# Leaving out the 45 dummy products per image on TensorE in an attention-and-FFT image block

## The chip, the cores and the metric

The kernel runs on one core of a Trainium2 chip. TensorE multiplies, VectorE (DVE), ScalarE (ACT) and GpSimd (POOL) work element by element, SyncE (SP) issues the transfers. The metric is the device time of one execution in microseconds: the median of the runs shown. [...]

## The reference

The input is eight images of 384 channels and 64 x 64 pixels. Two layers follow each other, each with a group norm before it and a residual after it:

```
x = x + linear_attention(group_norm(x))      # layer 0
x = x + fft_conv_gate(group_norm(x))         # layer 1

# layer 0, per image; q and k get rotary factors, 6 heads of 64
q = elu(rope(Wq x + bq) / 8) + 1 ;  k = elu(rope(Wk x + bk)) + 1 ;  v = Wv x + bv
kv = k^T v (per head) ; ksum = sum of k over pixels
out = Wfc (q kv / (q ksum + 1e-6)) + bfc

# layer 1, per image
t = W_in x ; t = irfft2(rfft2(t in 8x8 patches) * filter) ; t = depthwise 3x3(t)
out = W_out (gelu(t[:192]) * t[192:])

# group norm: 32 groups of 12 channels, mean and variance over channels and pixels
```

## The kernel before, in words

The images run one after the other in an unrolled program, and each is cut into 8 chunks of 512 pixels. An image has three parts.

Part A (`part_a`) takes each chunk in four tiles of 128 pixels. `project` multiplies the normalised image, split into a high and a low half (x_hi, x_lo), with the query, key and value weights (lines L1136, L1137, L1141). DVE turns (`rope`), ACT takes exponentials, POOL adds, DVE finishes the key tile (`elu`, L853), and `add_kv` (L1164) adds the product of keys and values, with the key sums in one column more, into one PSUM bank over the whole image.

Then comes the *key-value seam*. DVE copies the key sums (`ksum`, L883), makes diagonal matrices of them (`kdiag`, L887), and fixes the key-value matrix up (`kvfix`, L891, L895). TensorE spreads the key sums over all partitions with a product of ones (L1198); ACT copies that out as `kbc` (L607). TensorE transposes the fixed matrix (L1202), ACT copies it (L609), TensorE multiplies it by Wfc (L1207), and ACT and DVE split that into `mout_hi` and `mout_lo`. Beside it, POOL and DVE multiply the first chunk's queries by `kbc` (L474, L944), DVE sums them per head and takes reciprocals (L906 to L910), DVE and POOL divide (L917, L481), and TensorE transposes the divided queries (L1217).

Part B (`part_b`), the output stage, multiplies the transposed queries by `mout` for each chunk (L1238, L1246). DVE adds bias and residual and takes the statistics of the sum (L936, L968). POOL's divisions L481 come once per chunk.

Then comes the *statistics seam*, `group_norm` on DVE and `group_avg` on TensorE. Per channel means and variances are averaged over the channels of a group by two small products of two columns each (L1124): the first on the means (`mv`), read back in L794, the second on variance plus squared deviation (`dev`), read back in L799. DVE and ACT make the scale and the shift (L801 to L806), DVE normalises the first chunk for layer 1 (L823), ACT rounds it to x_hi (L567), DVE takes x_lo (L1027).

Part C (`part_c`) is layer 1: the projection (again L1136, L1137, L1141), the transform to the patch basis (L1283), the filter on DVE (L987), the way back (L1290), the taps of the depthwise convolution on ACT, POOL, DVE and TensorE (L1007, L1317), gates, and the output product (L1302 to L1306). Part A of the next image begins at its end.

Every engine takes its instructions in the written order and waits on semaphores, so a product that waits holds up all that are written behind it. `keep_warm` (L1113) writes products whose result nobody reads, of 128 rows by 512 columns, into a bank that is free at that time. They wait for nothing themselves. In each image 6 stand ahead of the last `add_kv`, 4 ahead of L1198, 2 ahead of L1202, 10 ahead of the first transposes of part B, 14 ahead of the first small product of `group_avg`, 2 ahead of its second, and 7 ahead of the first product of part C.

Of the kernel before, what the change touches and what calls it, by code (L numbers as in the profile page):

```python
# [10 lines left out]
P = 128  # L11
KB = C // P
CHUNK = 512
NCH = NTOK // CHUNK
# [98 lines left out]
def build_program(nc, x, wqkv_t, bqk, bv, wfc_t, bfc, filt, w_in_t, w_dw, w_out_t,  # L113
# [11 lines left out]
    with ctx:  # L125
        def sb(name, shape, dt=fp32):
            return ctx.enter_context(nc.sbuf_tensor(name, shape, dt))
# [12 lines left out]
        w_hi = sb("w_hi", [P, KB, 3 * C], fp32r)  # L140
# [5 lines left out]
        win_hi = sb("win_hi", [P, KB, C], fp32r)  # L146
# [64 lines left out]
        bank = [ctx.enter_context(nc.psum_tensor(f"bank{j}", [P, 512], fp32)) for j in range(8)]  # L211
# [75 lines left out]
        def steps(total, body):  # L287

            for c in range(total):
                body(c, c // 2, c, c % 2)  # L290

        def within(edge, a, b, off=0):

            return edge is None or a <= edge + off < b
# [810 lines left out]
        def _(pe):  # L1105
# [1 line left out]
            pe.wait_ge(s_cst, NCST * 16)  # L1107
            nc.tensor.matmul(bank[6][:, 0:C], sel, fsel[:, :], start=True, stop=True).then_inc(s_filter, 1)

            def keep_warm(n, free):  # L1110

                for _ in range(n):
                    nc.tensor.matmul(bank[free][:, :], win_hi[:, 0, 0:P], w_hi[:, 0, 0:CHUNK], start=True, stop=True)  # L1113

            def group_avg(f, n_warm=0, free=0):

                for step, (wait, src) in enumerate(((1, lambda k: mv[:, :, k, 0]), (4, lambda k: dev[:, :, k]))):
                    if step == 1:
                        keep_warm(n_warm, free)
                    pe.wait_ge(s_gs, f * 11 + wait)  # L1120
                    for m in range(KB):
                        ks = [k for k, mm in GBLOCKS if mm == m]
                        for k in ks:
                            ins = nc.tensor.matmul(bank[7][:, 2 * m:2 * m + 2], t_gavg[:, GBLOCKS.index((k, m)), :], src(k),  # L1124
                                                   start=(k == ks[0]), stop=(k == ks[-1]))
                    ins.then_inc(s_gp, 1)

            group_avg(0)
            pe.wait_ge(s_split, 2)

# [13 lines left out]
            def project(T, m, par, j, blocks=range(3)):  # L1144

                p2 = j % 2
                pe.wait_ge(s_rope, T + 1)
                pe.wait_ge(s_v, T + 1)
                tok = slice(j * P, (j + 1) * P)
                for b in blocks:  # L1150
                    dst = bank[ABANK[p2][b]][:, 0:C]
                    cols = slice(b * C, (b + 1) * C)
                    ins = split_product(dst, lambda k: x_hi[:, par, k, tok], lambda k: x_lo[:, par, k, tok],
                                        lambda k: w_hi[:, k, cols], lambda k: w_lo[:, k, cols],
                                        m if j == 0 and b == 0 else None)
                    ins.then_inc(s_qkv, 1)

            def add_kv(T, j, first=False, last=False, frees=False):

                pe.wait_ge(s_elu, T + 3)  # L1160
                pe.wait_ge(s_v, T + 3)
                p2 = j % 2
                for k in range(KB):
                    ins = nc.tensor.matmul(bank[KVB][:, k * (P + 1):(k + 1) * (P + 1)], kt[:, p2, k * P:(k + 1) * P],  # L1164
                                           vt[:, p2, k, :], start=(first and k == 0), stop=last, skip_group_check=True)
                    if frees and k == 0:
                        ins.then_inc(s_xfree, 1)
                ins.then_inc(s_kv, 1)
# [3 lines left out]
            for i in range(images):  # L1172

                def part_a(c, h, edge, par):
                    T = (i * 8 + c) * 4
                    first = edge == 0
                    m = i * 16 + c
                    project(T + 2, m, par, 2)
                    if first:
                        pe.wait_ge(s_res, i * 48 + 6)  # L1180
                    add_kv(T, 0, first=first)
                    project(T + 3, m, par, 3)
                    add_kv(T + 1, 1, frees=True)
                    if within(edge, 0, NCH, 1):
                        project(T + 4, m + 1, 1 - par, 0)
                    add_kv(T + 2, 2)
                    if within(edge, 0, NCH, 1):
                        project(T + 5, m + 1, 1 - par, 1)
                    if edge == NCH - 1:
                        keep_warm(6, 0)  # L1190
                    add_kv(T + 3, 3, last=(edge == NCH - 1))

                steps(NCH, part_a)


                keep_warm(4, 5)
                pe.wait_ge(s_kd, i * 5 + 2)
                nc.tensor.matmul(bank[0][:, 0:C], ones_r[:, :].bitcast(fp32), kdiag[:, :, :], start=True, stop=True).then_inc(s_kp, 1)  # L1198
                keep_warm(2, 5)
                pe.wait_ge(s_kd, i * 5 + 4)  # L1200
                for j in range(KB):
                    ins = nc.tensor.transpose(bank[1][:, j * P:(j + 1) * P], kvfix[:, j], ident)  # L1202
# [7 lines left out]
                def transpose_q(c, par, blocks=range(KB)):  # L1210
                    n = i * 8 + c
                    pe.wait_ge(s_qn, n + 2)
                    pe.wait_ge(s_qnp, n + 2)
                    for j in blocks:
                        pe.wait_ge(s_ql, n * 3 + (j + 1))
                        for u in range(TPC):
                            ins = nc.tensor.transpose(bank[(par + j) % 2][:, u * P:(u + 1) * P],  # L1217
                                                      qn[:, par, u, j * P:(j + 1) * P], ident)
                        ins.then_inc(s_tp, 1)

                keep_warm(10, 5)
                transpose_q(0, 0)
                pe.wait_ge(s_ka, i * 5 + 5)
                pe.wait_ge(s_mlo, i * 3 + 3)
# [35 lines left out]
                    if more:  # L1260
                        transpose_q(c + 1, 1 - par, (2,))
                steps(NCH, part_b)
                keep_warm(14, 0)
                group_avg(i + 1, 2, 0)
                keep_warm(7, 0)


                pe.wait_ge(s_split, 3)
# [139 lines left out]
```

## Time and profile before

| | us |
|---|---|
| median of 3 runs | 3549.17 |
| lowest, highest | 3548.68, 3550.89 |
| the profiled execution | 3545.66 |
| span of its trace | 3543.9 |

The profiled execution is one more run, 3.5 us below the median of the others. The span runs from its first to its last instruction. Of the span TensorE is busy 94%, DVE 84%, POOL 58%, ACT 49%. An image takes about 434 us. In this text image 0 is the first, and image 1 has its key-value seam near 668 us and its statistics seam near 750 us of the span.

In the trace's rows a time is microseconds from the span's start. Matmuls are pipelined, and each is shown with its own latency, so that two neighbours overlap; a product of fp32 operands has two records. Idle time before an instruction stands in brackets, with what ended it.

### The profile page before, as it was taken

What the parts mean: (1) busy time and instruction counts of PE and PEld (TensorE: products, weight loads), DVE (VectorE), ACT (ScalarE), POOL (GpSimd) and SP (SyncE); (2) the same over time, 40 slices, a digit from 0 to 9 for tenths busy, and PEclk for the clock granted to TensorE, in tenths of its full rate; (3) what the DMA queues carried; (4) which work ended last, traced back from release to release, by engine and by line L of the source; (5) the groups of instructions that cost most, each with busy time, mean ns of one, the idle gap of its engine ahead of it and who ended that gap; (6) DMA issues with size and microseconds to landing.
All of it is one profiled execution on the core that took longest, in us unless ns stands there. A gap on an engine that the chain in (4) does not pass through costs nothing. (4 is left out here: it accounts for less than half of the span.)

```text
span 3543.9 us, 50201 instructions
## 1 busy us (share of the span) xinstructions
PE 3318.6 (94%) x17374; PEld 2872.3 (81%) x17374; DVE 2981.3 (84%) x5231; ACT 1723.4 (49%) x3159; POOL 2042.9 (58%) x1343
## 2 busy tenths in 40 slices
PE   5999999999999999999999999998999999999998
PEld 4987779877797778977789777896779967799775
DVE  7877989779898798887989879888798887888887
ACT  2433854338443474435744257442664426644275
POOL 2555755547556475564755647456565565655665
PEclk9999999999999999999999999999999999999999
DMA  6215332143321432123332233213332133331422
GB/s 224 72 36 178 106 109 72 54 161 107 122 67 63 143 132 100 63 85 125 130 101 70 90 133 124 100 54 111 113 125 99 54 131 113 113 101 52 143 99 98
DMA packets 185341, 369.89 MB, mean 104 GB/s; under 512 B 7771, under 2 KB 8835, under 8 KB 184835
## 3 DMA queue, kind: packets, MB, share of 16 engines
q1 hardware_dynamic: 185090, 366.68, 30.3%
q8 instruction: 142, 2.33, 0.3%
q14 instruction: 109, 0.88, 0.1%
HBM read 265.99 MB, written 100.66 MB: 103 GB/s over the span
## 5 line engine op out<-in xcount | busy, mean ns | idle before, releaser
L1136 PE MATMUL bank<-w_hi,x_hi 128*128 128x384 f32 x2304 | 803.5, 349 | 17.9 <-ACT vt L578 10.7
L444 POOL TENSOR_TENSOR t<-t 128x768 f32<-128x768 f32 x256 | 535.3, 2091 | 466.4 <-DVE t L841 462.4
L1137 PE MATMUL bank<-w_lo,x_hi 128*128 128x384 f32 x2304 | 781.7, 339 | 0.0
L1007 DVE SCALAR_TENSOR_TENSOR bank<-big,wdw,bank 128x512 f32<-128x512 f32 x1072 | 749.1, 746 | 20.4 <-PE bank L1317 17.3
L437 POOL TENSOR_TENSOR x_lo<-xa,x_hi 128x512 fp32r<-128x512 f32 x360 | 459.4, 1292 | 478.4 <-ACT x_hi L567 478.4
L509 POOL TENSOR_TENSOR prod<-prod 128x512 f32<-128x512 f32 x320 | 410.5, 1283 | 244.5 <-ACT prod L670 224.9
L1141 PE MATMUL bank<-w_hi,x_lo 128*128 128x384 f32 x2304 | 533.1, 339 | 0.5 <-POOL x_lo L437 0.5
L572 ACT ACTIVATE t<-t 128x384 f32<-128x384 f32 x256 | 134.7, 526 | 759.5 <-POOL t L444 747.8
L1136 PEld LDWEIGHTS bank<-w_hi,x_hi 128*128 128x128 f32 x2304 | 436.8, 190 | 23.9 <-issue 22.7
L1137 PEld LDWEIGHTS bank<-w_lo,x_hi 128*128 128x128 f32 x2304 | 437.3, 190 | 1.1
L1141 PEld LDWEIGHTS bank<-w_hi,x_lo 128*128 128x128 f32 x2304 | 415.0, 189 | 1.4 <-POOL x_lo L437 1.4
L836 DVE TENSOR_TENSOR bank<-bank,qkbias 128x384 f32<-128x384 f32 x512 | 279.6, 559 | 137.9 <-PE bank L1141 137.6
L1136 PE MATMUL bank<-win_hi,x_hi 128*128 128x384 f32 x768 | 305.4, 398 | 0.9 <-ACT x_hi L567 0.4
L670 ACT ACTIVATE prod<-big,wdw 128x512 f32<-128x512 f32 x384 | 261.5, 715 | 71.5 <-DVE bank L1007 71.2
L1290 PEld LDWEIGHTS bank<-t_mats,gb 128*128 128x128 f32 x1536 | 205.4, 191 | 89.9 <-issue 35.5
L626 ACT ACTIVATE qt_hi<-bank 128x512 fp32r<-128x512 f32 x192 | 107.4, 594 | 314.8 <-PE bank L1217 314.8
L1137 PE MATMUL bank<-win_lo,x_hi 128*128 128x384 f32 x768 | 259.9, 338 | 0.0
L841 DVE TENSOR_TENSOR t<-bank,t_csw 128x384 f32<-128x384 f32 x512 | 258.4, 545 | 0.0
L1238 PE MATMUL bank<-qt_hi,mout_hi 128*128 128x512 f32 x576 | 247.7, 430 | 0.0
L1164 PE MATMUL bank<-vt,kt 128*128 128x129 f32 x1536 | 214.8, 275 | 25.6 <-DVE kt L853 25.6
L1290 PE MATMUL bank<-t_mats,gb 128*128 128x128 f32 x1536 | 217.1, 277 | 17.8 <-ACT big L640 9.4
L1164 PEld LDWEIGHTS bank<-vt,kt 128*128 128x128 f32 x1536 | 206.9, 190 | 30.6 <-DVE kt L853 30.6
(132 smaller groups left out, 6966.8 us busy)
## 6 DMA issues: line engine op xcount, KB each, us to landing
xr<-x SPq DMA_DIRECT2D x128, 768.0 KB, 4.7
xa<-x SPq DMA_DIRECT2D x64, 768.0 KB, 6.3
x_scratch<-xr SPq DMA_DIRECT2D x64, 768.0 KB, 3.3
xa<-x_scratch SPq DMA_DIRECT2D x64, 768.0 KB, 6.0
xr<-x_scratch SPq DMA_DIRECT2D x64, 768.0 KB, 4.8
out<-xr SPq DMA_DIRECT2D x64, 768.0 KB, 3.3
big<-x SPq DMA_DIRECT2D x8, 768.0 KB, 10.2
w_raw<-wqkv_t SPq DMA_DIRECT2D x1, 1728.0 KB, 6.8
```

The costliest lines, as they stand in the source:

```text
L437: nc.gpsimd.tensor_tensor(dst, src, hi, ALU.subtract).then_inc(s_lo, 1)
L444: nc.gpsimd.tensor_tensor(a, a, b[:, :, ::-1, :], ALU.add).then_inc(s_add, 1)
L509: nc.gpsimd.tensor_tensor(prod[:, 0], prod[:, 0], prod[:, slot_of(q)], ALU.add).then_inc(s_padd, 1)
L670: nc.scalar.activation(prod[:, slot_of(q)].rearrange("p (r s) -> p r s", s=W), filt_img[:, 2, ds(c * ROWS + q // 3, ROWS), q % 3:q % 3 + W ...
L836: nc.vector.tensor_tensor(qk, qk, qkbias[:, b * C:(b + 1) * C], ALU.add).then_inc(s_bias, 1)
L841: ins = nc.vector.tensor_tensor(dst[:, p2, b].rearrange("p s (f r) -> p s f r", r=2), src, tab.unsqueeze(1).unsqueeze(3).to_broadcast(wide ...
L1007: nc.vector.scalar_tensor_tensor(dst, src, wdw[:, k, q:q + 1], so_far, ALU.mult, ALU.add)\
L1136: nc.tensor.matmul(dst, hi(k), whi(k), start=(k == 0), stop=False)
L1137: nc.tensor.matmul(dst, hi(k), wlo(k), start=False, stop=False)
L1141: ins = nc.tensor.matmul(dst, lo(k), whi(k), start=False, stop=(k == KB - 1))
L1164: ins = nc.tensor.matmul(bank[KVB][:, k * (P + 1):(k + 1) * (P + 1)], kt[:, p2, k * P:(k + 1) * P], vt[:, p2, k, :], start=(first and k == ...
L1290: ins = nc.tensor.matmul(bank[INVB][:, k * P:(k + 1) * P], gb[:, p2, k * P:(k + 1) * P], phi_t, start=True, stop=True)
```

## The change

The function `keep_warm` and its seven calls go. `group_avg` loses the two arguments that only fed it. No other instruction is added, taken away or put elsewhere. The lines after it move up by 7 to 14 in the new file.

```diff
-            def keep_warm(n, free):
-
-                for _ in range(n):
-                    nc.tensor.matmul(bank[free][:, :], win_hi[:, 0, 0:P], w_hi[:, 0, 0:CHUNK], start=True, stop=True)
-
-            def group_avg(f, n_warm=0, free=0):
+            def group_avg(f):
 
                 for step, (wait, src) in enumerate(((1, lambda k: mv[:, :, k, 0]), (4, lambda k: dev[:, :, k]))):
-                    if step == 1:
-                        keep_warm(n_warm, free)
                     pe.wait_ge(s_gs, f * 11 + wait)
...
-                    if edge == NCH - 1:
-                        keep_warm(6, 0)
                     add_kv(T + 3, 3, last=(edge == NCH - 1))
 
                 steps(NCH, part_a)
 
 
-                keep_warm(4, 5)
                 pe.wait_ge(s_kd, i * 5 + 2)
                 nc.tensor.matmul(bank[0][:, 0:C], ones_r[:, :].bitcast(fp32), kdiag[:, :, :], start=True, stop=True).then_inc(s_kp, 1)
-                keep_warm(2, 5)
                 pe.wait_ge(s_kd, i * 5 + 4)
...
-                keep_warm(10, 5)
                 transpose_q(0, 0)
...
                 steps(NCH, part_b)
-                keep_warm(14, 0)
-                group_avg(i + 1, 2, 0)
-                keep_warm(7, 0)
+                group_avg(i + 1)
```

TensorE's written order at the key-value seam of the first image, before:

```order
L1164 MATMUL bank<-vt,kt 128x129 x6
L1113 MATMUL bank<-w_hi,win_hi 128x512 x6
L1164 MATMUL bank<-vt,kt 128x129 x3
L1113 MATMUL bank<-w_hi,win_hi 128x512 x4
L1198 MATMUL bank<-kdiag,ones_r 128x384
L1113 MATMUL bank<-w_hi,win_hi 128x512 x2
L1202 MATMUL bank<-t_mats,kvfix 128x128 x3
L1207 MATMUL bank<-wfc,kv_t 128x384 x3
L1113 MATMUL bank<-w_hi,win_hi 128x512 x10
L1217 MATMUL bank<-t_mats,qn 128x128 x12
```

And the same place now, with the new file's line numbers (L1157 is the old L1164, L1188 the old L1198, L1206 the old L1217):

```order
L1157 MATMUL bank<-vt,kt 128x129 x9
L1188 MATMUL bank<-kdiag,ones_r 128x384
L1191 MATMUL bank<-t_mats,kvfix 128x128 x3
L1196 MATMUL bank<-wfc,kv_t 128x384 x3
L1206 MATMUL bank<-t_mats,qn 128x128 x12
```

The four L1113 rows are gone, and the real products follow each other in the same order. At the statistics seam, before:

```order
L1246 MATMUL bank<-qt_lo,mout_hi 128x512 x3
L1113 MATMUL bank<-w_hi,win_hi 128x512 x14
L1124 MATMUL bank<-mv,t_gavg 128x2 x7
L1113 MATMUL bank<-w_hi,win_hi 128x512 x2
L1124 MATMUL bank<-dev,t_gavg 128x2 x7
L1113 MATMUL bank<-w_hi,win_hi 128x512 x7
L1136 MATMUL bank<-win_hi,x_hi 128x384
```

And now (L1234, L1117 and L1129 are the old L1246, L1124 and L1136):

```order
L1234 MATMUL bank<-qt_lo,mout_hi 128x512 x3
L1117 MATMUL bank<-mv,t_gavg 128x2 x7
L1117 MATMUL bank<-dev,t_gavg 128x2 x7
L1129 MATMUL bank<-win_hi,x_hi 128x384
```

Here three L1113 rows are gone, and between the last output product and the first product of layer 1 only the small products of two columns are left.

## Rows read from the trace of the kernel before

**Rows 1.** The page, part 1: busy us (share of the span) xinstructions.

```profile
PE 3318.6 (94%) x17374; PEld 2872.3 (81%) x17374; DVE 2981.3 (84%) x5231; ACT 1723.4 (49%) x3159; POOL 2042.9 (58%) x1343
```

**Rows 2.** The core's span and its mean granted TensorE clock.

```profile
core 0: 3543.9 us, clock 0.981
```

**Rows 3.** Stretches: length, busy us (instructions) per engine, granted clock, DMA share, GB/s.

```profile
668.30:671.70 3.40, 3.40 (x10) 2.41 (x10) 2.17 (x8) 0.00 (x0) 0.00 (x0) 0.50 0.00 1
682.00:685.30 3.30, 3.30 (x10) 2.75 (x11) 2.52 (x4) 0.60 (x1) 1.10 (x1) 0.50 0.02 5
747.00:753.60 6.60, 6.18 (x34) 4.88 (x33) 4.47 (x11) 0.00 (x0) 0.00 (x0) 1.00 0.52 179
753.60:760.50 6.90, 6.71 (x23) 5.16 (x22) 2.97 (x14) 0.97 (x3) 0.00 (x0) 0.51 0.57 204
487.40:490.80 3.40, 3.40 (x13) 3.40 (x12) 3.24 (x7) 1.89 (x3) 1.97 (x2) 0.50 0.48 186
700.00:740.00 40.00, 38.31 (x187) 29.35 (x187) 39.48 (x59) 10.91 (x20) 31.04 (x14) 1.00 0.55 185
1982.40:1989.20 6.80, 6.03 (x17) 4.87 (x17) 5.08 (x7) 1.07 (x2) 4.28 (x3) 0.50 0.00 0
```

The engines stand in the order PE, PEld (TensorE's weight loads), DVE, ACT, POOL.

**Rows 4.** TensorE in order of time, end of image 0: start, length, line, [idle before].

```profile
486.06 0.47 PE L1302 MATMUL bank<-g_hi,wout_hi 128*128 128x512 f32 x1 [3.55 <-DVE xr L939]
```

**Rows 5.** All engines in order of time, key-value seam of image 1.

```profile
668.45 2.06 PE L1113 MATMUL bank<-w_hi,win_hi 128*128 128x512 f32 x4
...
669.10 0.68 DVE L887 TENSOR_SCALAR kdiag<-t_mats,ksum 128x128 f32<-128x128 f32 x3
...
670.30 1.48 PE L1198 MATMUL bank<-kdiag,ones_r 128*128 128x384 f32 x2
...
671.82 0.49 ACT L607 ACTIVATE kbc<-bank 128x384 f32<-128x384 f32 x1 [5.25 <-PE bank L1198]
...
677.55 2.14 POOL L481 TENSOR_TENSOR qn<-big,nrm 128x768 f32<-128x768 f32 x1 [2.57 <-DVE nrm L910]
...
685.62 2.15 POOL L481 TENSOR_TENSOR qn<-big,nrm 128x768 f32<-128x768 f32 x1 [2.52 <-DVE nrm L910]
...
693.93 2.15 POOL L481 TENSOR_TENSOR qn<-big,nrm 128x768 f32<-128x768 f32 x1 [0.55 <-DVE nrm L910]
```

**Rows 6.** The same in image 4.

```profile
1973.10 0.49 ACT L607 ACTIVATE kbc<-bank 128x384 f32<-128x384 f32 x1 [4.04 <-PE bank L1198]
...
1978.82 2.15 POOL L481 TENSOR_TENSOR qn<-big,nrm 128x768 f32<-128x768 f32 x1 [2.57 <-DVE nrm L910]
...
1986.89 2.15 POOL L481 TENSOR_TENSOR qn<-big,nrm 128x768 f32<-128x768 f32 x1 [2.52 <-DVE nrm L910]
...
1996.42 2.15 POOL L481 TENSOR_TENSOR qn<-big,nrm 128x768 f32<-128x768 f32 x1 [0.55 <-DVE nrm L910]
```

**Rows 7.** Statistics seam of image 1, in order of time.

```profile
751.58 1.72 PE L1124 MATMUL bank<-mv,t_gavg 128*128 128x2 f32 x14 [0.42 <-DVE mv L790]
...
754.10 3.15 PE L1124 MATMUL bank<-dev,t_gavg 128*128 128x2 f32 x14
...
757.36 0.17 DVE L799 TENSOR_SCALAR gvar<-bank 128x6 f32<-128x6 f32 x1 [3.31 <-PE bank L1124]
...
760.51 0.41 PE L1136 MATMUL bank<-win_hi,x_hi 128*128 128x384 f32 x1
...
765.01 0.91 PE L1283 MATMUL bank<-tb,t_mats 128*128 128x384 f32 x2 [0.59 <-ACT tb L634]
```

**Rows 8.** The second small product's reader at the statistics seam of image 2.

```profile
1190.37 0.17 DVE L799 TENSOR_SCALAR gvar<-bank 128x6 f32<-128x6 f32 x1 [1.89 <-PE bank L1124]
```

**Rows 9.** Who waited for whom: us in total, times, longest us.

```profile
ACT kbc L607 <- PE bank L1198: 37.4, 8, 5.3
DVE gvar L799 <- PE bank L1124: 27.1, 9, 3.3
DVE gmean L794 <- PE bank L1124: 18.5, 9, 3.3
```

## The prediction

> **What bounds the kernel now.** I read the page's busy shares first. TensorE is busy 94% of the span [rows 1], but that counts pipelined products and the dummies too. So I asked for busy times by stretch. In the middle of the output stage VectorE is busy 39.48 of 40 us, TensorE 38.31 [rows 3]: VectorE sets the pace there, and little on TensorE's side is worth anything. The change touches only the two seams of an image, where this does not hold: the key-value seam, between the last projection and the first output product, and the statistics seam, between the last output product and the first product of the second layer. There one engine works at a time, and small products stand in the chain.
>
> Next, TensorE's granted clock. [...] Even with the dummies it falls at the seams: in image 1 from 668.3 to 671.7 and again from 682.0 to 685.3 as the output stage starts, and at the statistics seam from 753.6 to 760.5 [rows 3]. The mean over the span is 0.981 [rows 2], so low time is about 2 x 0.019 x 3544 = 135 us. A fall also comes with no dummy near: TensorE idles 3.55 us before L1302 at 486.06 [rows 4], and from 487.4 to 490.8 the clock is 0.50 [rows 3]. So idleness brings it down, and the dense work that follows brings it back 3 to 5 us after it begins (682.0 to 685.3, and 486.1 to 490.8). The fall at 487.4 came 4.9 us after that idle stretch began. I reckon with falls 2 to 6 us after dense work ends, an estimate around this one and the others at the seams.
>
> **The change part by part.** Removed are 6 + 4 + 2 + 10 dummies at the key-value seam and 14 + 2 + 7 at the statistics seam, in each of eight images. Nothing is added, and the order of everything else stays. The direct saving is small, since the dummies fill waits. Only where the clock is low do they hold something up: in image 1 the four at 668.45 run low, and L1198 starts at 670.30, though its diagonal was ready at 669.10 + 0.68 = 669.78 [rows 5]. That 0.5 us is in term 1. The others end before what they stand ahead of is ready; L1136 at 760.51 [rows 7] waits for its x_hi anyway. What the change costs is the clock, in five terms.
>
> 1. *The way to the key row, kbc.* The chain is: last key tile, product into the key-value bank, sums, diagonal, L1198, ScalarE's copy L607. From there to the first division on POOL (L481) the way is fixed: 677.55 - 671.82 = 5.73 us in image 1, 1978.82 - 1973.10 = 5.72 in image 4 [rows 5, 6]. ScalarE idles before L607 5.25 us in image 1, where the clock is low, and 4.04 in image 4, where it is not [rows 5, 6]; 37.4 over eight, 4.68 on average [rows 9]. Without dummies only two short products into the bank stand between the projections and L1198, so I expect a low clock in all eight. Of image 1's 5.25, 0.5 goes with the dummies; its low set in at 668.3 only, with the product into the bank partly done (a dummy behind it starts at 668.45), and a wholly low one adds, I estimate, up to 0.6. That makes 5.4. Cost 0.75 x 8 = 6 us. Ends: 0 and 1.1 each, 9.
>
> 2. *Start of the output stage.* TensorE now comes to it low in every image. Image 1 was low for 3.3 us there, and its divisions on POOL follow each other after 8.07 and 8.31 us. Image 4 was low for 6.8 us (1982.4 to 1989.2), and they follow after 8.07 and 9.53 [rows 3, 5, 6]. So a short low is free and a long one costs 1.2; the first kind is the commoner at the seams before. After, between both: 0.5 each, 4 us, less the 1.2 paid already: 2.8. Ends: -1.2 and 8 x 1.2 - 1.2 = 8.4.
> [...]
>
> 3. *First statistics step.* Fourteen records of two columns each take 1.72 us at full clock (751.58) and 3.15 low (754.10) [rows 7]; VectorE waits for them in L794. Over nine such waits it idles 18.5 us [rows 9], 2.06 each, near the 1.89 of a step at full clock (L799 in image 2 [rows 8]): with 14 dummies ahead this step is mostly at full clock. Four dummies take 2.06 us at the low level [rows 5], so about 0.22 each at full clock; 14 of them and the 0.42 idle behind them are some 3.5 us, in which TensorE now does nothing. With falls 2 to 6 us after dense work, about half the images take the step wholly low and most others partly: 1.0 of the 1.43 each, 8.0 us. Ends 0 and 11.4.
>
> 4. *Second statistics step.* VectorE waits 3.31 us before L799 in image 1 (low), 1.89 in image 2 (full), 27.1 over nine [rows 7 to 9]. One of the nine lies ahead of the images and is as long as the longest, 3.3, so eight make 23.8. All low: 26.5. Cost 2.7, nearly fixed.
>
> 5. *Start of the second layer.* The 7 dummies bring the clock back at 760.5, just when the first product comes [rows 3, 7]. Without them real products must do it, in 3 to 6 us. The first 2 us are hidden, since the products wait for x_hi and x_lo. Up to 4 us at half speed then lose up to 2, and TensorE's idle 0.59 before L1283 takes part of it [rows 7]: 0 to 1.5 each. As in term 2 a short low is free and a long one dear; I take 0.7, 5.6 us. Ends 0 and 12. It is kept afterwards, because VectorE only waits here and is the bound later.
>
> Sum: 6 + 2.8 + 8 + 2.7 + 5.6 = 25 us. The profiled execution took 3545.66 us, so 3571 in its terms. The median of the runs stands 3.5 us above it: 3549.2 + 25 = 3574.
>
> **Rivals.** I call a difference real over 0.2%, 7 us: about what a measurement of this kernel can tell from none.
>
> *A. The lows fall where nothing waits.* Image 1's second low was free. Then only term 4 and part of term 1 are left, 3 to 6 us: 3552 to 3555. Against it: at both statistics steps VectorE waits for TensorE with nothing else to do, in every image.
>
> *B. The clock falls from load, and the dummies bring it down.* The lows at 668.3 and 753.6 do set in among dummies [rows 3, 5]. Without them both seams would run at full clock: L607 waits 4.04 instead of 4.68 (-5.1 us), L799 1.89 instead of 2.98 (-8.7), the output stage's 1.2 goes: -15, so 3534, faster. It decides if the seams show 1.00. Against it: rows 4, a fall after plain idleness, and 40 us of dense products at 1.00 in rows 3.
>
> *C. Every low microsecond costs half of one.* By rows 3 the lows at image 1's seams sum to 3.4 + 3.3 + 6.9 = 13.6 us. They would grow to about 27: from the last key tile to some 4 us into the output stage with a recovery between, and from 4 us after its end to 4 us into the next layer. 13 x 8 / 2 = 52 us, 3601. Against it: image 1's low at the output stage cost nothing, and TensorE mostly waits while it is low.
> [...]
>
> **How the numbers follow.** Forecast 0.78, A 0.10, B 0.04, C and all above 3591 0.08. Slower by over 0.2%: 0.86; within: 0.10; faster: 0.04. The range: with terms 1 and 3 at half, 2 and 5 near nothing and 4 whole, 3 + 4 + 2.7 = 10, I go a little below that, to 3556, to take in part of A; with 2, 3 and 5 near their upper ends (5, 3 and 6 more, and 3 for term 1), 3574 + 17 = 3591. So 3556 to 3591.
>
> **What would show it.** Mean clock 0.961 to 0.970, low time some 100 us more than 135. L607's idle about 5.4 us in every image, none near 4.0, 43 over eight. L794's wait for the statistics product grows from 18.5 to about 26, L799's from 27.1 to about 29.8. The second layer's first L1283 comes up to 1.5 us later after L1136. The output stage goes on at 8.3 us a chunk. I am wrong if the statistics steps show full clock, if the added waits are there but the stages behind them shorten by as much, or if the second layer absorbs term 5.

## The result, and the profile after

| | before | changed |
|---|---|---|
| median, us | 3550.03 (4 runs, 3548.68 to 3552.57) | 3578.66 (4 runs, 3577.01 to 3584.52) |
| ratio, 95% interval | | 1.0083 [1.0065, 1.0100] |
| span of the profiled execution | 3543.9 | 3582.7 |
| mean granted clock of TensorE | 0.981 | 0.956 |

The change costs 28.6 us, 0.8%. The profiled execution of the changed kernel was the slowest of its four runs, and that of before stood below its median, so the two traces differ by 38.8 us, ten more than the medians. Up to seven of those ten can be put down to longer waits for loads, shown below.

The page's first lines, to be held against [rows 1]:

```profile
span 3582.7 us, 49481 instructions
PE 3278.2 (91%) x17014; PEld 2850.6 (80%) x17014; DVE 2985.9 (83%) x5231; ACT 1724.6 (48%) x3159; POOL 2042.3 (57%) x1343
```

TensorE lost 360 products and 40 us of busy time, and the other engines have the same number of instructions as before. Stretches of image 1 (its seams now stand 6 and 7 us later), columns as in [rows 3]:

```profile
661.00:673.00 12.00, 7.81 (x50) 7.42 (x48) 8.34 (x18) 4.59 (x9) 4.15 (x2) 1.00 0.19 51
673.00:683.30 10.30, 8.15 (x17) 4.24 (x17) 5.69 (x13) 2.06 (x5) 2.48 (x1) 0.50 0.05 19
683.30:686.70 3.40, 0.96 (x8) 0.86 (x8) 2.37 (x5) 0.63 (x2) 3.20 (x2) 1.00 0.00 0
686.70:693.50 6.80, 5.76 (x18) 4.59 (x17) 5.09 (x7) 1.45 (x3) 4.28 (x2) 0.50 0.00 0
758.40:775.50 17.10, 12.48 (x47) 12.34 (x48) 6.90 (x23) 3.98 (x9) 3.07 (x3) 0.50 0.55 186
```

The lows of 3.4, 3.3 and 6.9 us have become 10.3, 6.8 and 17.1. In this trace the granted clock reads 1.00 or 0.50 in every half microsecond from 662 to 702 us but the four in which it changes (0.56, 0.70, 0.72 and 0.96); 0.50 is what is called low here. The key-value seam is at the low level from the last key tile to the end of the Wfc products, comes back for 3.4 us, in which TensorE is nearly idle, and falls again among the transposes: eight of the twelve begin at 685.74, the last four at 687.85. All engines there, in order of time, against [rows 5]:

```profile
673.40 1.66 PE L1157 MATMUL bank<-vt,kt 128*128 128x129 f32 x6 [3.40 <-DVE kt L853]
...
676.09 1.65 PE L1188 MATMUL bank<-kdiag,ones_r 128*128 128x384 f32 x2 [1.04 <-DVE kdiag L887]
...
677.78 0.49 ACT L607 ACTIVATE kbc<-bank 128x384 f32<-128x384 f32 x1 [5.49 <-PE bank L1188]
...
678.96 4.21 PE L1196 MATMUL bank<-wfc,kv_t 128*128 128x384 f32 x6 [0.58 <-ACT kv_t L609]
...
683.50 2.15 POOL L481 TENSOR_TENSOR qn<-big,nrm 128x768 f32<-128x768 f32 x1 [2.57 <-DVE nrm L910]
...
691.57 2.15 POOL L481 TENSOR_TENSOR qn<-big,nrm 128x768 f32<-128x768 f32 x1 [2.52 <-DVE nrm L910]
...
700.93 2.15 POOL L481 TENSOR_TENSOR qn<-big,nrm 128x768 f32<-128x768 f32 x1 [0.55 <-DVE nrm L910]
```

ScalarE waits 5.49 us for the key row, and the way from there to the first division is 5.72 as before. The Wfc products take 4.21 us instead of 2.20, and that costs nothing: what reads them is due later. POOL's second division follows the first after 8.07 us, and the third the second after 9.36. At the statistics seam of the same image, against [rows 7]:

```profile
758.96 3.15 PE L1117 MATMUL bank<-mv,t_gavg 128*128 128x2 f32 x14 [4.00 <-DVE mv L790]
...
762.22 0.16 DVE L794 COPY gmean<-bank 128x6 f32<-128x6 f32 x1 [3.31 <-PE bank L1117]
...
762.90 3.15 PE L1117 MATMUL bank<-dev,t_gavg 128*128 128x2 f32 x14 [0.79 <-DVE dev L797]
...
766.16 0.17 DVE L799 TENSOR_SCALAR gvar<-bank 128x6 f32<-128x6 f32 x1 [3.31 <-PE bank L1117]
...
769.32 0.66 PE L1129 MATMUL bank<-win_hi,x_hi 128*128 128x384 f32 x1 [3.27 <-ACT x_hi L567]
...
775.22 0.93 PE L1269 MATMUL bank<-tb,t_mats 128*128 128x384 f32 x2
...
776.24 0.56 DVE L987 TENSOR_TENSOR gb<-bank,fsel 128x384 f32<-128x384 f32 x1 [3.71 <-issue]
```

Both small products now take the low 3.15 us. From the first product of layer 1 to L1269 (the old L1283) it is 5.90 us instead of 4.50, and TensorE no longer idles before it. The waits summed over the program, against [rows 9]:

```profile
ACT kbc L607 <- PE bank L1188: 44.0, 8, 5.5
DVE gvar L799 <- PE bank L1117: 29.8, 9, 3.3
DVE gmean L794 <- PE bank L1117: 28.7, 9, 3.3
DVE bn_x L872 <- DMA xr<-x: 16.3, 7, 3.2
DVE xr L936 <- DMA xr<-x: 5.0, 8, 1.8
```

The last two are VectorE's waits for loads of x. Before they were

```profile
DVE bn_x L872 <- DMA xr<-x: 11.5, 7, 1.8
DVE xr L936 <- DMA xr<-x: 2.8, 8, 0.5
```

so 7.0 us of the 38.8 are longer waits for loads. For the start of layer 1 the measure is VectorE's idle time before its filter product L987. It is the part of the answer called "issue" (the profile shows nothing that ended the wait), and its eight waits are those of the first tile of each image. Before:

```profile
  issue: 18.3, 8
```

and after:

```profile
  issue: 24.6, 8
```

### The profile page after: what moved, and what is told of

It is laid out like the page before. It is cut to its first block, busy times and chain, and to the rows that moved or that the text cites. A ratio compares the mean times of both kernels' runs of the same rounds, so it can differ in the third digit from the quotient of the medians.

```text
span 3582.7 us, 49481 instructions
## 1 busy us (share of the span) xinstructions
PE 3278.2 (91%) x17014; PEld 2850.6 (80%) x17014; DVE 2985.9 (83%) x5231; ACT 1724.6 (48%) x3159; POOL 2042.3 (57%) x1343
## 4 chain that ended last, share of the span: by engine, by line
PE 67%; DVE 18%; issue 5%; POOL 4%; ACT 3%; DMA 2%; SPq 0%; DVEq 0%; POOLq 0%; ACTq 0%
PE bank L1129 14%; PE bank L1134 14%; PE bank L1130 14%; PE bank L1157 5%; PE bank L1269 4%; PE bank L1276 4%; DVE bank L1007 3%; PE bank L1303 3%; DVE nrm L906 3%; DVE qt_lo L926 3%; DVE xr L936 2%; PE bank L1288 2%; PE bank L1117 2%; POOL prod L509 1%; DVE bn_x L968 1%
## 5 line engine op out<-in xcount | busy, mean ns | idle before, releaser
L1129 PE MATMUL bank<-w_hi,x_hi 128*128 128x384 f32 x2304 | 804.7, 349 | 21.7 <-ACT vt L578 10.1
L1129 PEld LDWEIGHTS bank<-w_hi,x_hi 128*128 128x128 f32 x2304 | 437.9, 190 | 27.6 <-issue 26.5
L1129 PE MATMUL bank<-win_hi,x_hi 128*128 128x384 f32 x768 | 310.4, 404 | 26.1 <-ACT x_hi L567 26.1
L1157 PE MATMUL bank<-vt,kt 128*128 128x129 f32 x1536 | 220.0, 280 | 36.7 <-DVE kt L853 36.7
L1157 PEld LDWEIGHTS bank<-vt,kt 128*128 128x128 f32 x1536 | 211.2, 194 | 40.3 <-DVE kt L853 40.3
L1226 PE MATMUL bank<-qt_hi,mout_lo 128*128 128x512 f32 x576 | 234.5, 407 | 0.0
```

Source lines behind the costliest of these rows:

```text
L1129: nc.tensor.matmul(dst, hi(k), whi(k), start=(k == 0), stop=False)
L1226: nc.tensor.matmul(bank[2 + 3 * par + m][:, :], w[:, j, m * P:(m + 1) * P], qt_hi[:, par, j], start=(j == 0 and w is mout_hi), stop=False)
```

## The experiments

Times are medians, each against runs of the kernel before made beside it on the same chip, in three groups. The medians of before were 3549.49 (15 runs), 3551.04 (12) and 3548.53 (21). The line numbers of a variant are its own. The divisions in question are POOL's L481, one for each chunk; "the first filter products" are the first L987 of each image.

**Half of the dummies: the key-value seam.**

```diff
-                    if edge == NCH - 1:
-                        keep_warm(6, 0)
...
-                keep_warm(4, 5)
...
-                keep_warm(2, 5)
...
-                keep_warm(10, 5)
```

> Only the 22 dummies of the key-value seam (6 + 4 + 2 + 10) are left out; the 23 of the statistics seam stay. Theory (idleness lowers the clock, and the loss is the sum of the stages that wait for TensorE while it is low): the way from the last key tile to the first division costs 18.22 us in every image instead of 17.41 on average (+6.5 us over eight), the next division interval grows by 0.65 each (+5.2): +12 us, time 3562. The waits of L794 and L799 stay as before (18.5 and 27.1 us within 2). Rival (one long low stretch is carried from seam to seam, so that the loss does not split): the statistics seam is slower too, and the time is nearer to that of the change, 3570 or more.

3561.66, ratio 1.0038 [1.0025, 1.0052], +12.2 us. The waits:

```profile
ACT kbc L607 <- PE bank L1195: 44.0, 8, 5.5
DVE gvar L799 <- PE bank L1124: 28.4, 9, 3.3
DVE gmean L794 <- PE bank L1124: 18.4, 9, 3.3
```

L607 waits as in the changed kernel, L794 as before, L799 1.3 us more. From the end of the last key tile to the first division it is 10.15 us in every image. The 18.2 us that the expectations give "to the first division" reach to the second one, 8.07 us later; the differences between kernels are the same either way. The interval from the second division to the third grew by 6.3 us over eight. The rival of a low that is carried from seam to seam falls.

**The other half: the statistics seam.**

```diff
-                keep_warm(14, 0)
-                group_avg(i + 1, 2, 0)
-                keep_warm(7, 0)
+                group_avg(i + 1, 0, 0)
```

> Only the 23 dummies of the statistics seam (14 + 2 + 7) are left out; the 22 of the key-value seam stay. Theory: L794's wait +10 us over eight, L799's +2.8, the start of the second layer +6.3: +19 us, time 3569; the key-value seam stays as before (L607's wait 37.4 us within 2). Rival (the loss does not split): under 3562 or over 3576. The two halves together should make the change's own +29 to +31.

3563.94, ratio 1.0047 [1.0035, 1.0060], +14.5 us where 19 were expected.

```profile
ACT kbc L607 <- PE bank L1198: 38.5, 8, 5.3
DVE gvar L799 <- PE bank L1124: 29.8, 9, 3.3
DVE gmean L794 <- PE bank L1124: 25.3, 9, 3.3
```

L794's wait rose by 6.8, not 10: it depends on when the clock falls after the last output product, and here it fell 5.2 to 5.3 us after it in four images and 2.0 to 2.7 us after it in the other four. L987's idle rose by 8.5 us, but the ends of layer 1 (from the last filter product to the last residual) were 2.8 us shorter. The two halves make 12.2 + 14.5 = 26.7, a little under the 29 to 31 expected and against 28.6 for the change: within the intervals the loss splits by seam.

**Dummies without columns.**

```diff
-                    nc.tensor.matmul(bank[free][:, :], win_hi[:, 0, 0:P], w_hi[:, 0, 0:CHUNK], start=True, stop=True)
+                    nc.tensor.matmul(bank[free][:, 0:2], win_hi[:, 0, 0:P], w_hi[:, 0, 0:2], start=True, stop=True)
```

> All 45 dummies stay, but each has 2 columns instead of 512; weight loads stay whole. Theory (the clock is held by streamed columns, not by the presence of instructions): as the change, 3575 to 3582, mean clock 0.955 to 0.960, L607's wait near 43 us. Rival (any products issued hold the clock, as weight loads do count): as before, 3550, mean clock 0.98.

3573.83, ratio 1.0071 [1.0059, 1.0084]. All 360 dummies are there, with their weight loads, and the mean clock is 0.957. The waits read almost as the changed kernel's:

```profile
ACT kbc L607 <- PE bank L1198: 43.6, 8, 5.5
DVE gmean L794 <- PE bank L1124: 28.6, 9, 3.3
```

So the mere presence of the instructions, weight loads among them, does not hold the clock. This run alone does not say that the streamed columns do, for thin dummies also fill less time. In image 1 (before: 3.42 us for the fourteen, and 0.42 idle behind them):

```profile
751.30 1.62 PE L1113 MATMUL bank<-w_hi,win_hi 128*128 128x2 f32 x14
...
755.33 1.97 PE L1124 MATMUL bank<-mv,t_gavg 128*128 128x2 f32 x14 [2.41 <-DVE mv L790]
```

The wide statistics products below part the two. The time lies 1 us under the expected range, which came from the changed kernel's slower profiled run.

**Only the last seven left out, twice.**

```diff
-                keep_warm(7, 0)
```

> Only the 7 dummies ahead of the second layer's first product are left out. Theory: L794's and L799's waits stay as before; the clock comes back only by the real products, and the way from L1136 to the first filter product L987 grows from 5.5 us to between 5.5 and 6.9: +3 to +6 us, time 3553 to 3556. Rival (the second layer absorbs a late start): 3550 within 2 us, though the clock is low for as long.

> The kernel without the last seven dummies again, since its first trace showed 4.8 us more at the start of the second layer and its median only 0.8. Theory (the term is kept to the end): 3 to 5 us over the kernel before in the median. Rival (it is absorbed or was the luck of one trace): within 2.

3550.30 (11 runs), ratio 1.0007 [0.9999, 1.0016], and 3549.61 (11 runs), 1.0001 [0.9992, 1.0011]. Both lie below what I expected (3 to 6 and 3 to 5 us over before) and within the rival's range. The mechanism is in both traces all the same: the clock comes back 3.0 to 6.1 us after the first product of layer 1, and the first filter products come 4.8 and 4.4 us later over eight images (L987's issue time in the second is 23.2). But the end of layer 1 gives some of it back: in images with a late start the way from the last filter product to the last residual is 35.1 us, in images with a punctual one around 35.7 (in all kernels between 34.6 and 36.4). There too the clock can fall once more (as at 487.4 in [rows 3]); that the shift decides what it falls on is my reading and was not tested. The medians leave about 1 us, under what can be told. The two traces show 5 and 6 us over their counterparts. So the term is real where it arises, and how much of it reaches the end stays open between 0 and 5 us.

**Only the last seven kept** at the statistics seam (14 and 2 out):

```diff
-                keep_warm(14, 0)
-                group_avg(i + 1, 2, 0)
+                group_avg(i + 1, 0, 0)
```

> At the statistics seam only the 7 last dummies stay (14 + 2 left out), the key-value seam as before. Theory: L794's wait +7 to +10 us and L799's +2.8 as without all 23, but the second layer starts as before (44 to 45 us over eight from its first product to the first filter product): +10 to +12, time 3560 to 3562, and 3 to 5 under the kernel without all 23.

3561.81, ratio 1.0040 [1.0027, 1.0053], +13.3 us. L987's issue time is back at 18.3, L794's wait 26.2, L799's 29.8. Against the kernel without all 23 the first filter products come 8.5 us earlier over eight, the ends of layer 1 are 4.3 us longer, and the excess over before is 13.3 instead of 14.5 us, a difference within both intervals. The time lies in the expected 3560 to 3562, but the 3 to 5 us under the kernel without all 23 were missed, in the same way as with the last seven left out. The give-back shows here from the other side.

**Both kernels again**, for a second trace of each:

> The kernel before, unchanged, for a second trace and more runs. Theory (the first layer's chunks and the loads are the same in every kernel here, and what differs there between traces is scatter): the way from each image's last residual to the next image's last key tile sums to 1204 us over seven, within 4. The key-value and statistics waits differ from the first trace by a few us only, as the lows fall at other moments. 3550 within 3.

> The changed kernel, unchanged, for a second trace. The first one was the slowest of four runs and had 6.3 us more than before in the projection parts of seven images, with longer waits of VectorE for loads. Theory (scatter of the transfers, not the clock): the second trace has less of it, 1204 to 1208, while the seams repeat: 18.2 us to the first division in each image, L794 and L799 as in the first trace. 3578 within 3. Rival (the low clock disturbs the loads as well): again 6 us more there.

Before: 3546.20 (11 runs, 3542.45 to 3551.74), ratio 0.9995 [0.9986, 1.0004]; that is 0.8 us under the expected range and 2.3 under the 21 runs of the same kernel beside it, so differences of 2 us between medians say nothing here. Changed: 3577.19 (3574.67 to 3578.75), ratio 1.0082 [1.0069, 1.0096]. In the second trace of the changed kernel L607 waits 43.5, L794 and L799 29.8 each; the waits for loads are

```profile
DVE bn_x L872 <- DMA xr<-x: 12.9, 7, 3.2
DVE xr L936 <- DMA xr<-x: 4.6, 8, 1.6
```

The projection parts took 1206.8 us instead of the first trace's 1210.2; before they took 1203.9 and 1204.9, and in the variants 1204.6 to 1208.1. So most of the first trace's excess there was scatter. Not all of it need be: in both traces of the changed kernel one and the same stretch, from image 4's last residual to image 5's last key tile, is some 3 us longer than most, and no such stretch of another kernel is over 1.7 longer. The 2 us of L936 came in both traces of the changed kernel and once more without any dummies (4.6 us, the kernel below with wide products and none), while all kernels with dummies have 1.8 to 3.4. Why the loads are later then is open.

**Wide statistics products.** Each of the two columns is streamed 64 times, and VectorE reads one of each 64:

```diff
-                            ins = nc.tensor.matmul(bank[7][:, 2 * m:2 * m + 2], t_gavg[:, GBLOCKS.index((k, m)), :], src(k),
+                            ins = nc.tensor.matmul(bank[7][:, P * m:P * m + P].rearrange("p (s r) -> p s r", s=2),
+                                                   t_gavg[:, GBLOCKS.index((k, m)), :],
+                                                   src(k).unsqueeze(2).to_broadcast([P, 2, P // 2]),
...
-                pm = bank[7][:, 0:2 * KB].rearrange("p (m s) -> p s m", s=2)
+                pm = bank[7][:, 0:P * KB].rearrange("p (m s r) -> p s m r", s=2, r=P // 2)[:, :, :, 0]
```

> Before, with the 45 dummies, but the small products of the group statistics stream 128 columns (each of the two columns repeated 64 times) instead of 2; VectorE reads one column of each 64. Theory: the small products now hold the clock themselves; seven of them take the same 1.7 us at full clock since their weight loads set their pace, so L799's wait falls from 27.1 to about 19 over nine and nothing else changes: -8 us, 3542. Rival (the products get longer by their columns, 0.2 us each and more): L794 and L799 both wait longer, 3550 to 3560.

3539.57 (9 runs), ratio 0.9975 [0.9965, 0.9985], -11.5 us.

```profile
DVE gmean L794 <- PE bank L1124: 19.3, 9, 3.4
DVE gvar L799 <- PE bank L1124: 17.9, 9, 2.0
```

And image 1's statistics seam, its two steps and the clock over them:

```profile
749.71 1.83 PE L1124 MATMUL bank<-mv,t_gavg 128*128 128x128 f32 x14 [0.53 <-DVE mv L790]
...
752.34 1.83 PE L1124 MATMUL bank<-dev,t_gavg 128*128 128x128 f32 x14 [0.33 <-DVE dev L797]
```

```profile
747.00:753.60 6.60, 5.74 (x37) 4.55 (x36) 3.05 (x10) 0.00 (x0) 0.00 (x0) 1.00 0.70 225
753.60:760.50 6.90, 5.26 (x28) 3.95 (x27) 5.68 (x16) 2.55 (x6) 0.00 (x0) 1.00 0.34 130
```

L799's wait fell by 9.2 us, for 0.8 more in L794. Here the same products with the same weight loads take nearly the same time as before (1.83 instead of 1.72 us) and differ in the columns alone, and the clock stays at 1.00 from the last output product to the first product of layer 1, in every image. That is what shows that streamed columns, and not only filled time, hold it.

**The same in the changed kernel**, without dummies:

> The changed kernel (no dummies at all) with group products of 128 columns. Theory: the clock is low when the group products begin, after nearly 4 us of idleness, and 1.7 us of products do not bring it back at once: L794's wait stays or grows (each product is twice as long when low, and 128 columns in four passes last 0.43 us, 3 us for seven), L799's gains little: within 5 us of the change, 3574 to 3584. Rival (the small products alone were the loss at this seam): 3565 or less.

3573.27, ratio 1.0068 [1.0055, 1.0081]: L794 31.1, L799 24.0. The time is 0.7 us under the expected range. The wide products did not take away a low that was already on when they began. In four of eight images that low lasts 3.4 us, L799 waits 1.99 us and the second step is at full clock; in the other four it lasts 17.1 us, and L799 waits 3.52. Each of their products has two records in the traces, and what the expectation calls four passes shows in the time alone: at the low level three products of 384 columns with plain fp32 operands (L1196 of the changed kernel) take 4.21 us, 1.40 each, and those with rounded operands (L1132 here) start 0.32 us apart, a quarter of that or a little less. A wide step that is low throughout takes 3.36 us.

**More dummies at the same places.**

```diff
-                        keep_warm(6, 0)
+                        keep_warm(13, 0)
...
-                keep_warm(10, 5)
-                transpose_q(0, 0)
+                keep_warm(18, 5)
+                transpose_q(0, 0, (0, 1))
+                keep_warm(4, 5)
+                transpose_q(0, 0, (2,))
...
-                keep_warm(14, 0)
+                keep_warm(16, 0)
...
-                keep_warm(7, 0)
+                keep_warm(12, 0)
```

> Before with more dummies at the same places (13, 4, 2, 18 and 4 more between the two groups of transposes at the key-value seam; 16, 2, 12 at the statistics seam). Theory: the clock stays full through the key-value seam in nearly all images: L607's wait falls from 37.4 to about 33 us, the output stage's long low goes: -4 to -6 us; at the statistics seam the small products still bring it down and the 12 dummies at the low level (0.43 us each, 5.1 us) then hold up the first product of layer 1 by some 1.8 us each, +10 or more: 3550 to 3560 in all. Rival (more dummies only delay): the key-value seam gets slower too, over 3565.

3537.41, ratio 0.9965 [0.9952, 0.9978], -13.6 us, where 3550 to 3560 were expected: I was wrong by 12.6 us or more. The key-value seam did as expected (L607 waits 32.3 us over eight, 4.0 each). The statistics seam, in image 1:

```profile
755.97 4.58 PE L1113 MATMUL bank<-w_hi,win_hi 128*128 128x512 f32 x12
...
756.22 0.17 DVE L799 TENSOR_SCALAR gvar<-bank 128x6 f32<-128x6 f32 x1 [1.89 <-PE bank L1124]
...
759.33 1.89 DVE L1027 TENSOR_TENSOR x_lo<-xa,x_hi 128x512 fp32r<-128x512 f32 x3
...
760.39 0.34 PE L1136 MATMUL bank<-win_hi,x_hi 128*128 128x384 f32 x1
```

The twelve do run partly low and hold the first product back by 1.0 us (L799 to L1136 takes 4.17 instead of 3.15; 1.2 more on average over eight), but that product's group ends with x_lo, which VectorE makes until 761.2: the delay is hidden, and L987's issue time is 19.1. And with 16 dummies ahead the clock fell later in five of eight images (6.3 to 9.1 us after the last output product, where it was 5.3 to 8.4 before), and L799's wait sank to 22.8.

**Both together.**

> The dummies of the kernel with more dummies, and the group products of 128 columns. Theory: full clock through both seams, -5 at the key-value seam and -8 at L799, no delay by the 12 dummies, as they run at full clock: 3537, mean clock over 0.99. Rival (wide products are no faster or the dummies delay): 3550 or more.

3535.76 (3535.09 to 3538.99), ratio 0.9962 [0.9949, 0.9975], -15.3 us against the kernel before and some 43 us, 1.2%, against the changed one.

The mean clock is 0.993. Stretches of image 1:

```profile
664.00:682.00 18.00, 16.69 (x78) 11.83 (x77) 10.22 (x21) 5.85 (x12) 8.64 (x4) 1.00 0.14 45
753.60:760.50 6.90, 6.41 (x34) 4.99 (x34) 4.38 (x14) 1.88 (x4) 0.00 (x0) 1.00 0.50 181
```

And the waits:

```profile
ACT kbc L607 <- PE bank L1200: 32.3, 8, 4.0
DVE gvar L799 <- PE bank L1124: 19.5, 9, 3.5
```

Both seams stand at full clock. This is the fastest version measured. Whether it needs both its parts can't be told: the intervals of the last three faster versions overlap.

## Why the prediction was right, point by point

Forecast 3574 in 3556 to 3591; measured 3578.66. The mechanism is settled by three things: the seams are low where the dummies are gone, dummies with the same weight loads but two columns do not help, and small products that last nearly as long but stream more columns keep the clock up and take waits away that before had.

The terms over eight images, from the first traces of both, with the second pair in brackets:

| term | forecast | measured |
|---|---|---|
| 1. last key tile to the divisions | 6 | 6.5 (9.9) |
| 2. start of the output stage | 2.8 | 5.2 (4.7) |
| 3. first statistics step | 8 | 10.2 (11.4) |
| 4. second statistics step | 2.7 | 2.7 (4.1) |
| 5. start of layer 1 | 5.6 | 6.3 (4.1) |

*Term 1.* L607 idles 5.49 us in all eight, where 5.4 was worked out from a low row, less its dummies, plus a product wholly at the low level. The second bracket is larger because before itself scatters: its second trace had L607 waiting 33.5 us instead of 37.4.

*Term 2* was the most mis-sized: 5.2 us where 2.8 was forecast. I put 0.5 between a free low of 3.3 us and a dear one of 6.8. In the changed kernel the clock comes back only after 6.8 us of it in image 1, and the second interval between divisions is 8.5 to 9.5 us in every image of the first trace, 0.65 more on average than before. The trace lies between the forecast and the upper end of 8.4: the clock falls at 686.7 in the middle of the transposes, and image 1's low ends 4.9 us after the first dense product. No run here has transposes alone ahead of that stage, so what they do for the clock stays open.

*Term 3* was taken too small: seven of eight images, not half, took the step wholly low. Its base was right for another reason than given: the 2.06 us of the average hold the step ahead of the images (3.32), and in the eight images L794 waited 1.88 to 2.03, always at full clock. I had reckoned with falls 2 to 6 us after dense work. In the changed kernel seven of eight came 2.3 to 3.6 us after the last output product and one 5.3; the step begins 3.8 to 4.2 us after it (5.4 in the last image).

*Term 4* came out exactly in the first pair: L799 29.8 where about 29.8 was written.

*Term 5* arises as said (24.6 - 18.3 = 6.3), but that it is kept to the end was wrong in part: 0.8 us in the first pair and 3.4 in the second come back at the ends of layer 1, and the runs without the last seven could not show a loss in the median. One of the three signs that I had named for being wrong, layer 1 absorbing this term, thus came true in part.

Sum of the five: 30.9 in the first pair, 34.2 in the second, where 25 was forecast; four of the five came out larger. They account for the traces, not for the medians. In the first pair 30.9, less 0.8 given back in layer 1, plus 6.3 in the projection parts and 2.2 of L936's waits for loads, make 38.6 of the 38.8 us between the spans; in the second 34.2 - 3.4 + 1.9 + 2.7 = 35.4, against 34.8. The medians say 28.6 and 28.7, and the difference lies in which executions were profiled: both of the kernel before are among its faster ones (3545.7 and 3543.9, where its runs lie between 3541.1 and 3554.3), and both of the changed kernel are the slowest of their four. By the medians the forecast sum was 3.6 us too small, by the traces' terms 6 to 9. That it came as near as it did owes something to luck: terms 2 and 3 were too small, the give-back at the end of layer 1 was left out, and the two errors offset each other.

*Rival A*, lows where nothing waits, was true of the Wfc products and false of the rest. *Rival B*, load brings the clock down, is refuted by every run: fewer dummies always gave a lower clock (0.956 to 0.977), more gave a higher one (0.989, 0.993). Its price for full clock at both seams was right all the same: it said -15 us, and the kernel with more dummies and wide products, where both seams are at full clock, measured -15.3. *Rival C*, half a microsecond for each low one, would ask for (314 - 137) / 2 = 89 us by the low time that the mean clocks give (0.044 x 2 x 3583 = 315 us against 135, the 2 because the low level reads 0.50). A third of that was lost. TensorE is not idle while it is low (it is busy in 26.4 of the 34.2 low us of image 1 above), but much of what it does more slowly there nobody waits for, such as the Wfc products. My 0.961 to 0.970 for the mean clock was too high: I had the lows at 235 us in sum, not 315. At the statistics seam they last 13.7 to 17.1 us, and those of the key-value seam 17.1 to 20.5 in sum (first trace), where I had taken about 27 for both together.

## What to carry to other kernels

Where engines take turns in a short chain, price TensorE's idleness by what the clock does to the small products in the chain (here 3.15 us a step instead of 1.72) and to the first dense ones behind it, and ask for each low stretch who waits for TensorE in it; the share of low time says little. Filler products belong in waits that exist already, and here they had to stream columns: with two columns each the time was 3573.83, ratio 1.0071. Beside fillers, where weight loads set the pace (they fill 1.64 of the 1.72 us of a statistics step), the real small products can stream more columns, which cost 0.11 us a step here. They do not replace the fillers: without any dummies the wide products left the kernel 0.7% slower than before.

## What the runs showed of the hardware that was not expected

- A statistics step of 14 records takes 1.72 us with 2 columns and 1.83 with 128, at full clock. In the kernel with wide products and the 45 dummies L799's longest wait was 2.0 us, so the clock stood in every second step; with two columns it fell before or within that step in seven of eight images of the first trace, though weight loads were issued one after the other.
- Twelve dummies, partly at the low level, that delay a product by 1.2 us on average cost nothing in the end, because the group that it opens ends with an operand that comes later still.
- The kernel before scatters by 13 us over 48 runs, the one with a mean clock of 0.993 by 4 us over 5. That falls of the clock cause the scatter is not shown: the kernel without the key-value dummies, at 0.967, also stayed within 4.2 us over its 5 runs.
